# Outer products by pair of heads, the carry on VectorE, routing tables in 16 bits, constants loaded behind the input

## What is computed

```
x = x + 0.5 * ffn(layernorm(x));  x = x + attn(layernorm(x));  x = x + 0.5 * ffn(layernorm(x))

ffn(x):  e = argmax(x @ Wr.T + br)                  # one of 8 experts per token
         relu(x @ W1[e].T + b1[e]) @ W2[e].T + b2[e]        # 128 -> 512 -> 128

attn(x): q, k, v = silu(x @ Wq), silu(x @ Wk), silu(x @ Wv)   # 16 heads of 8, chunks of 128 tokens
         per chunk:  o  = ((q k^T) * mask) v + lam_q * (q @ kv)     # mask: exp(-s (i-j)), j <= i
                     kv = lam_c * kv + (k * lam_k)^T v              # carried to the next chunk
         (layernorm(o) * gamma + beta) * sigmoid(x @ Wg1 @ Wg2) @ Wo
```

## Time and profile before

| | us |
|---|---|
| median of 3 runs (452.79 to 458.83) | 452.91 |
| the profiled execution, its time | 454.72 |
| its span, first to last instruction | 452.7 |

### The profile page before, as it was taken

One profiled execution on the slowest core, in us unless ns is written; L12 is line 12 of the kernel. 1 busy time (PEld: TensorE's weight loads), 2 busy tenths in 40 slices (PEclk: granted clock), 3 DMA queues, 4 the chain that ended last, 5 costly groups with the idle time before them and its releaser, 6 DMA issues.

```text
span 452.7 us, 10251 instructions
## 1 busy us (share of the span) xinstructions
PE 364.9 (81%) x2508; PEld 325.6 (72%) x2508; DVE 293.9 (65%) x996; ACT 195.9 (43%) x586; POOL 294.2 (65%) x306
## 2 busy tenths in 40 slices
PE   4966999999988977886859889852388999999930
PEld 4955988999977765765657767732387988999920
DVE  3594567444464886685949898897856677666510
ACT  2552663555545232435344745413065434555500
POOL 0006772763886699989787898910277777777771
PEclk9999999999999999696969999995669999999985
DMA  7736787787861000001010101101278855776510
GB/s 230 268 94 203 226 234 183 217 202 217 222 181 30 20 6 17 4 16 46 20 47 1 47 2 46 46 2 46 74 215 241 202 185 161 219 209 198 159 35 0
DMA packets 41303, 54.00 MB, mean 119 GB/s; under 512 B 6212, under 2 KB 25818, under 8 KB 40992
## 3 DMA queue, kind: packets, MB, share of 16 engines
q1 hardware_dynamic: 34496, 39.49, 27.8%
q0 software_dynamic: 6176, 13.26, 12.2%
...
...
## 4 chain that ended last, share of the span: by engine, by line
PE 48%; POOL 23%; DVE 11%; issue 10%; DMA 3%; DVEq 1%; ACT 1%; POOLq 1%; ACTq 0%
PE bank L1238 15%; PE bank L1228 15%; POOL outer_all L301 9%; PE bank L1287 5%; POOL rows L404 4%; POOL qS L461 4%; PE bank L1190 3%; PE bank L1184 2%; PE bank L1266 2%; PE bank L1220 2%; PE bank L1322 2%; POOL out_x L423 1%; DMA const_sb<-in_const 1%; DVE outer_all L895 1%; POOL rows L411 1%
## 5 line engine op out<-in xcount | busy, mean ns | idle before, releaser
L390 POOL DMA_INDIRECT ring<-rows_d,token_in x92 | 88.1, 957 | 98.2 <-DVE token_in L906 71.4
L1228 PE MATMUL bank<-slot_xT,w_ring 128*128 128x128 f32 x736 | 104.7, 285 | 5.3 <-DVE hT_b L946 4.4
L1228 PEld LDWEIGHTS bank<-slot_xT,w_ring 128*128 128x128 f32 x736 | 94.6, 199 | 8.5 <-DVE hT_b L946 6.2
L1287 PE MATMUL bank<-outer_all,decay_sb 128*128 128x256 f32 x256 | 69.5, 397 | 14.6 <-POOL outer_all L301 12.6
L946 DVE TENSOR_SCALAR hT_b<-bank,b_cur 128x128 f32<-128x128 f32 x184 | 55.9, 345 | 38.5 <-PE bank L1228 32.8
L1287 PEld LDWEIGHTS bank<-outer_all,decay_sb 128*128 128x128 f32 x256 | 48.5, 198 | 32.0 <-POOL outer_all L301 13.8
L1238 PE MATMUL bank<-w_sb,hT_a 128*128 x368 | 60.6, 288 | 3.7 <-issue 0.9
L301 POOL TENSOR_TENSOR outer_all<-qkv 128x512 f32<-128x512 f32 x60 | 62.6, 1069 | 1.5 <-ACT qkv L613 1.4
L575 ACT ACTIVATE hT_a<-bank,b_cur 128x128 f32<-128x128 f32 x184 | 57.5, 364 | 12.9 <-PE bank L1228 12.4
L1238 PE MATMUL bank<-w_sb,hT_b 128*128 x368 | 56.8, 277 | 0.0
L423 POOL DMA_INDIRECT out_x<-ring,token_out x46 | 46.7, 1014 | 14.0 <-issue 12.5
...
## 6 DMA issues: line engine op xcount, KB each, us to landing
...
ring<-rows_d,token_in POOLq DMA_INDIRECT x92
...
```

Source lines behind the costliest of these rows:

```text
L390: pool.indirect_dma_start(n_in_ring(G) if layer_of(G) == 0 else in_ring(G), None, rows_d[u], bass.IndirectOffsetOnAxis(ap=token_in[u][:, j ...
L1228: last = mm(to[:, f * P:(f + 1) * P], w1_ring[G % W1_BUFS][:, (2 * half + f) * P:(2 * half + f + 1) * P], slot_xT[G % 2][:, :], start=True ...
L1287: last = mm(to, decay_sb[:, (2 * h + a) * P:(2 * h + a + 1) * P], u, start=True, stop=True)
```

## The change

Five parts:

1. `qkv` is laid out anew: q per batch, then k and v by head and batch. ACT writes it with two activations per batch (k and v, 256 wide; q, 128 wide) in place of one of 384. An outer-product instruction now does one pair of heads for all 4 batches (still 512 elements), and each has its own semaphore count, so that `state_product` of a pair waits for its pair alone. POOL does all eight of turn 0 itself (DVE did four of them, `first_outer`); in turn n it does pairs 5 to 7, and ahead pairs 0 to 4 of turn n+1.
2. The carry: `age_carry` on ACT and both POOL instructions go. DVE does `mask_delta` (PSUM times mask, back to PSUM) and `update_carry` (carry times decay plus PSUM), both of 512 elements, at the start of each turn from turn 1 on. `half_sum` now also helps in turn 7 (7 of 8 pairs). The fetches back are spread 2, 3, 3, 2, 2 over turns 0 to 4.
3. The turn's end: PE does `route_product` ahead of `out_transpose`, DVE the router's bias ahead of `gate`; in turn 7 `gate` moves behind `route_onehot` of unit 2, and PE's `out_product` of step 6 and `route_transpose` of step 5 ahead of `invert`.
4. Routing: the one-hot table is written in bf16 at once, its counts are read from PSUM where they are used (two copies go), and the tables for the inversion are all bf16 with the tiles innermost; a table `lane_by_tile` is written once by ACT in four parts at the start. PE's `invert` reads weights and moving operand with a stride of 20 (or 12) elements. The hooks of units 1 and 3 are one or two slots earlier.
5. Start: ACT loads `ident` and `lane` alone; the other constants are issued by SP behind x's step 4. The product of ones and router weights moves on PE from step 0 to step 3. `y_sb` and `b1_rows` now share other buffers' memory.

```diff
-                      ("prefer", EXPERTS), ("lane", P), ("tile_id", TOKEN_TILES), ("row_id", 1)):
+                      ("prefer", EXPERTS), ("tile_id", TOKEN_TILES), ("row_id", 1)):
...
-        helped = lambda n, h: n < STEPS - 1 and h % 4 != 3
+        helped = lambda n, h: h < PAIRS - 1 and (n == STEPS - 1 or h != 3)
...
+        BACK_IN_TURN = (2, 3, 3, 2, 2)
+        ADDED_IN_TURN = {1: SPLIT[0][0], 3: SPLIT[0][0] + 1, 4: SPLIT[0][0] + 2}
...
                 sp.dma_start(x_of_step(c), x_v[:, c]).then_inc(x_loaded[c], 16)
+                if c == SPLIT[0][0] - 1:
+                    sp.dma_start(const_sb[:, EARLY_W:CONST_W], const[:, EARLY_W:CONST_W]).then_inc(const_loaded, 16)
...
+            def outer_part(n, h):
+
+                if n == STEPS:
                     return
-                pool.wait_ge(qkv_done, BATCH * n + b + 1)
+                pool.wait_ge(qkv_done, BATCH * (n + 1))
                 wait(pool, state_ready, PAIRS * (n - 1))
-                ins = outer_product(pool, n, half, b)
-                if b == BATCH - 1:
-                    ins.then_inc(outer_done, 1)
+                flat = lambda part: part(n % 2)[:, 2 * h:2 * h + 2].rearrange("p h b e -> p (h b) e")
+                k_ = flat(k_of).unsqueeze(3).to_broadcast([P, 2 * BATCH, HD, HD])
+                v_ = flat(v_of).unsqueeze(2).to_broadcast([P, 2 * BATCH, HD, HD])
+                pool.tensor_tensor(outer[n % 2][:, h * PW:(h + 1) * PW].rearrange("p (a d e) -> p a d e", d=HD, e=HD),
+                                   k_, v_, ALU.mult).then_inc(outer_done, 1)
...
+            def split_qkv(s, b):
+                act.wait_ge(qkv_ready, BATCH * s.n + b + 1)
+                from_ = bank[3 + b % 2]
+                nc.scalar.activation(kv_by_head(s.par)[:, :, b], from_[:, D:3 * D].rearrange("p (c e) -> p c e", e=HD), ACT.Silu)
+                nc.scalar.activation(q_of(s.par, b), from_[:, 0:D], ACT.Silu).then_inc(qkv_done, 1)
...
                 chain.link(nc.vector.tensor_tensor(
-                    in_slot[:, 0:tiles * slots].rearrange("p (i s) -> p i s", s=slots),
-                    cst("lane")[:, 0:slots].unsqueeze(1).to_broadcast([P, tiles, slots]),
-                    hi.unsqueeze(2).to_broadcast([P, tiles, slots]), ALU.is_equal))
+                    in_slot[:, 0:tiles * slots].rearrange("p (s i) -> p s i", i=tiles), lanes_of(0, slots)[:, :, 0:tiles],
+                    hi.unsqueeze(1).to_broadcast([P, slots, tiles]), ALU.is_equal))
...
+            def mask_delta(n):
+
+                dve.wait_ge(delta_ready, n + 1)
+                nc.vector.tensor_tensor(per_batch(bank[6][:, :]), per_batch(bank[6][:, :]),
+                                        cst("carry_mask").unsqueeze(1).to_broadcast([P, BATCH, D]),
+                                        ALU.mult).then_inc(delta_masked, 1)
+
+            def update_carry(n):
+
+                dve.wait_ge(delta_masked, n + 1)
+                dve.wait_ge(carry_done, n + 1)
+                nc.vector.scalar_tensor_tensor(out=carry[:, :], in0=carry[:, :], scalar=cst("decay_c"), in1=bank[6][:, :],
+                                               op0=ALU.mult, op1=ALU.add).then_inc(carry_done, 1)
...
+                lanes = in_lane[:, 0:P * tiles].rearrange("p (l i) -> p l i", i=tiles)
+                ids = in_slot_id[:, 0:width * tiles].rearrange("p (w i) -> p w i", i=tiles)
                 for i in range(tiles):
-                    last = mm(counts_bank[:, PLACED_AT:PLACED_AT + width], in_lane[:, i * P:(i + 1) * P],
-                              in_slot_id[:, i * width:(i + 1) * width], start=(i == 0), stop=(i == tiles - 1))
+                    last = mm(counts_bank[:, PLACED_AT:PLACED_AT + width], lanes[:, :, i], ids[:, :, i],
+                              start=(i == 0), stop=(i == tiles - 1))
...
-                if s.n == 0 and h == 0:
-                    pe.wait_ge(first_outer_done, 1)
-                if s.n > 0 or h >= PAIRS // 2:
-                    pe.wait_ge(outer_done, 2 * s.n + h // (PAIRS // 2))
+                pe.wait_ge(outer_done, PAIRS * s.n + h + 1)
...
-                if r == 0:
+                if r == 3:
                     pe.wait_ge(const_loaded, 16)
                     mm(bank[7][:, 0:EXPERTS], cst("ones"), wr_sb[:, :], start=True, stop=True).then_inc(wr_summed, 1)
```

286 lines of the change are left out of this document (128 added, 158 removed).

## The result

The changed kernel takes 429.1 us (median of four executions, 426.96 to 430.97) where the kernel before takes 452.9: a ratio of 0.944, 95% interval 0.935 to 0.954. Forecast were 431.0 and "faster". The profiled execution took 426.96 us, span 424.9. Measured once more beside the last experiments, the changed kernel took 431.25 (six executions, 430.32 to 431.58) against 453.3, ratio 0.951 (0.948 to 0.955). I call the profile of that second measurement the yardstick; the experiments are mostly read against it.

The account below looks back on a forecast made before the run. POOL's 92 transfers (118 us) end the kernel unchanged, so only time before 324.25 us can pay. Gains 4.3 + 1.0 + 9.4 + 3.3 + 1.7 + 2.3 = 22.0 give 432.7 profiled, 431 median; range 422 to 442.

Parts of the forecast that it names:

- Start: Kernel start: PE no longer waits for the constants and continues 2.7 us earlier, less 0.60 for the moved product: 2.1 gained.
- One-hot and copies: First routing on DVE: the cast goes, 0.27 us, and two copies of 160 elements go, 0.57 us.
- Tables: First routing on DVE: all-bf16 tables take 1.49 us for 2560 elements and 0.44 for 540, 1.9 gained.
- Strided operands of `invert`: Both routings on PE: reading weights with a step of 40 bytes makes each inversion 0.5 us late, bounds 0 to 3.
- First pass and turn 0's earlier start: First expert pass gains 1.0 us by shorter hooks; attention's turn 0 begins at 147.4 instead of 148.66.
- Attention: Seven intervals between turns 0 and 7 sum to 133.7 us instead of 141.8, each set by the busier of DVE and POOL.
- The bound at DVE's floor: Attention intervals at DVE's busy time alone, 111.3 + 9.8 = 121.1 us, would gain 22.
- 4 x 0.75 = 3: Attention from turn 3 on: router products ahead of the output's transposes make gate 0.75 us later per turn, 3 us in all.
- Last turn: Turn 7: seven sums over d fall from 1.06 to 0.57-0.59 us, as POOL is idle: 3.3 gained.
- DVE closed up: Attention; rival that DVE keeps 3.5 us idle per turn: intervals sum to 144, median 441; chance 0.13.
- the rival's 6: Both inversions on PE: strided weights at the float32 price, 2 x 2.5 = 5 us less gained, median 436; chance 0.09.
- the slower case: Attention: POOL's outer products on the new layout take twice 1.04 us, 41 us lost there, median about 482; chance 0.03.

Follow-up runs that it names:

- b1: Kernel before with only the new qkv layout and an outer product per pair, POOL doing all eight of turn 0: 449.4 us, ratio 0.993.
- b2: Kernel before with only the carry masked and updated by DVE, ACT's and POOL's four operations gone: 447.1 us, ratio 0.985.
- e1: Changed kernel with the lane table's 128 lanes innermost again, all 16 bit, so invert's weights are contiguous: 433.4 us, ratio 0.957.
- e6: Changed kernel with slot tables in groups of two tiles, and DVE doing join twice in each turn: 426.8 us, ratio 0.942.
- e4: Changed kernel with the turn's end in the old order, out_transpose ahead of route_product and gate ahead of the bias: 426.8 us, ratio 0.943.
- the last version: Changed kernel with old turn's-end order except in turn 7, slot tables in groups of two, one-hot table in float32 then cast: 424.3 us, ratio 0.935.
- e8: Changed kernel with POOL doing kd twice in turns 0 to 6 and adding no halves in turn 7: 435.9 us, ratio 0.960.

## Why the prediction was right, and where it was not

The total is right to 2 us, and to 0.3 against the yardstick. By its steps, measured on the yardstick:

- *Start, 2.1 forecast.* The first routing step came 2.24 earlier (21.92 to 19.68). The 5.1 of the first profile is 2.2 plus 2.9 that PE's clock gave in that execution. The mechanism is right; that the number is too is partly luck, since b1 and b2 give 0.6 and 1.4 for the same gain. I had read the wait for the constants from one execution and taken its length for fixed.
- *One-hot and copies, 0.84 forecast.* The cast's 0.27 turned into a loss of 0.16: a 16-bit write with a stride takes 0.85, where 32-bit write and cast took 0.67. I had priced the cast and not the write that replaces it.
- *Tables, 1.9 forecast.* 1.48 and 0.44, as taken. e1 shows what it hangs on: no operand may repeat one element along the innermost dimension.
- *Strided operands of `invert`, 0.5 each.* The step that failed. DVE waited 1.44 and 2.05 us for PE, where before it waited nothing and 0.39, so each cost 1.4 to 1.7. I looked only at the weights. Alone they cost 0.33 in routing 1 (1.41 against 1.08) and 0.04 in routing 2, so my 0.5 was no bad price for them; most of the cost was in the moving operand, which I put at nothing without a reason, and which hides that of the weights. With that and the one-hot, routing 2 gained 1.0 instead of 2.3, and the first gather 3.1 instead of 4.3.
- *First pass and turn 0's earlier start, 2.26 forecast*: 2.2.
- *Attention, 8.1 forecast for the seven intervals*: 10.75. (The bound at DVE's floor added 1.4 for seven turns where the change adds it to six, so 121.1 should read 119.7; the range hardly moves.) Turn 0 was mis-sized, 19.3 for 21.0; turns 1 to 6 are within 0.5 each. In turns 3 to 6 the number was right but its reason only half: "the larger of DVE's sum and POOL's" leaves DVE 1.2 to 1.8 us idle per turn, and e6 shows that DVE's own work can grow at little cost. What I priced as an extra on DVE, `gate` waiting about 1.05 (measured 1.00), is the visible end of a chain over PE and ACT that sets the turn. Its price, 4 x 0.75 = 3, was right: e4 and the last version gave 2.7 and 2.8.
- *Last turn, 3.3*: 4.2, of which 3.05 are the half sums (e8), the rest no part of the forecast. *End of turn 7, 1.7*: 1.8. *Tail, nothing*: 0.4 to 1.1 shorter.

Of the rivals, DVE closed up well enough. The strided operands came out at 3.1 us for both routings, between my 1 and the rival's 6. Outer products on the new layout take 1.06 each, as before (1.07), so the slower case had nothing to stand on. The terms that were too large (routing, by 2.5) and too small (the intervals by 2.65, last turn and tail by 1.3) nearly cancelled; part of the closeness is luck.
